# SyncE's program of a graph network's three score passes, written out without its loop

## What is computed

```python
# layer 0: attention logits for 4 heads
a = einsum('ehd,ehd->eh', q[src], k[dst]) / sqrt(32)      # then a softmax over the edges of dst
# layer 1: an edge weight from a small network
h = gelu(concatenate([x[src], x[dst]]) @ mlp_w1 + mlp_b1)
edge_weight = sigmoid(h @ mlp_w2 + mlp_b2)
# layer 3: additive attention for 4 heads
e = leaky_relu(e_l[:, src] + e_r[:, dst], 0.2) + log(clip(w))
# all: out = segment_sum(weight * value[src], dst)
```

## Time and profile before

| what | value |
|---|---|
| median of three runs | 8695.56 us |
| profiled execution, its own time | 8723.79 us |
| its span | 8722.0 us |
| first, second, third score pass | about 121 to 1476, 2175 to 3491 and 6870 to 8201 us of the span |
| busy time: POOL, PE, DVE, ACT | 4695.0 us (54%), 3867.5 (44%), 3291.5 (38%), 2042.4 (23%) |
| granted TensorE clock over the span | 0.641 of full speed |
| DMA queue of SyncE (hardware_dynamic, q1) | 798344 packets, 452.32 MB |
| DMA queue of GpSimd (software_dynamic, q0) | 159744 packets, 356.39 MB |

### The profile page before, as it was taken

The page is one execution under the profiler, slowest core; times in us unless marked ns, Lnnn a source line. Parts: engine busy times, 40 slices in busy tenths (PEclk is TensorE's granted clock), DMA queues, the critical chain, the costliest instruction groups (busy, mean ns, idle before and its releaser), DMA issues. The chain is left out here.

```text
span 8722.0 us, 99954 instructions
## 1 busy us (share of the span) xinstructions
PE 3867.5 (44%) x22250; PEld 3542.3 (41%) x22250; DVE 3291.5 (38%) x8047; ACT 2042.4 (23%) x3881; POOL 4695.0 (54%) x5007
## 2 busy tenths in 40 slices
PE   4333333463666666666433333433333444444356
PEld 2333333352556555565332323422323433433246
DVE  4222223776344444776322222322222311111376
ACT  1000000583333333897000000000000200000067
POOL 2656564350666666232466666466665356665344
PEclk8666666796665666778656556655555655555589
DMA  5555554351444444564111111111111233333244
GB/s 148 162 161 166 161 158 134 96 154 34 125 123 125 123 126 123 173 196 137 44 45 45 45 45 41 48 44 45 46 44 39 58 83 84 88 85 83 61 125 140
DMA packets 973113, 863.79 MB, mean 99 GB/s; under 512 B 350004, under 2 KB 837256, under 8 KB 972808
## 3 DMA queue, kind: packets, MB, share of 16 engines
q1 hardware_dynamic: 798344, 452.32, 18.8%
q0 software_dynamic: 159744, 356.39, 15.8%
q10 hardware_dynamic: 14976, 54.53, 1.9%
HBM read 669.20 MB, written 193.56 MB: 99 GB/s over the span
## 5 line engine op out<-in xcount | busy, mean ns | idle before, releaser
L774 POOL DMA_INDIRECT sum_rows<-tab_row,sum_idx x1664 | 1578.7, 949 | 631.6 <-issue 551.2
L393 PE MATMUL l_pK<-l_winr,l_hotT 128*128 128x128 f32 (+2 forms) x4992 | 1040.4, 374 | 1774.0 <-ACT l_hotT L435 863.0
L393 PEld LDWEIGHTS l_pK<-l_winr,l_hotT 128*128 128x128 f32 x4992 | 993.2, 304 | 1856.8 <-issue 1412.4
L911 DVE TENSOR_TENSOR acc<-acc,sum_pA 128x128 f32 x4160 | 991.4, 289 | 1949.6 <-DMA att<-in_L_gnn_a_r 894.5
L808 PE MATMUL sum_pA<-sum_hot,sum_rows 128*128 128x128 f32 x3328 | 773.9, 426 | 1678.9 <-DMA sum_rows<-tab_row,sum_idx 1639.9
L808 PEld LDWEIGHTS sum_pA<-sum_hot,sum_rows 128*128 128x128 f32 x3328 | 720.7, 329 | 1732.2 <-issue 874.1
L375 POOL DMA_INDIRECT l_rows<-tab_ax,l_idx x832 | 811.2, 975 | 316.5 <-issue 266.5
L375 POOL DMA_INDIRECT l_rows<-tab_qv,l_idx x832 | 791.5, 951 | 316.4 <-issue 259.6
L375 POOL DMA_INDIRECT l_rows<-tab_wh,l_idx x832 | 789.5, 949 | 316.3 <-issue 278.1
L808 PE MATMUL sum_pA<-sum_hot,sum_wrow 128*128 128x128 f32 x4992 | 723.9, 305 | 358.3 <-DVE sum_hot L261 238.4
L808 PEld LDWEIGHTS sum_pA<-sum_hot,sum_wrow 128*128 128x128 f32 x4992 | 662.6, 214 | 408.4 <-issue 264.3
(11 more groups left out here) (235 smaller groups left out, 4464.9 us busy)
## 6 DMA issues: line engine op xcount, KB each, us to landing
spill<-l_rows SPq DMA_DIRECT2D x312, 512.0 KB
sum_rows<-spill SPq DMA_DIRECT2D x312, 512.0 KB
l_winr<-tab_k SPq DMA_DIRECT2D x840, 64.0 KB
sum_line<-src_lo ACTq DMA_DIRECT2D x104, 512.0 KB, 4.6
l_winr<-tab_b SPq DMA_DIRECT2D x840, 32.0 KB
sum_rows<-tab_row,sum_idx POOLq DMA_INDIRECT x1664
l_winr<-tab_er SPq DMA_DIRECT2D x840, 2.0 KB
l_rows<-tab_qv,l_idx POOLq DMA_INDIRECT x832
```

The costliest lines, as they stand in the source:

```text
L393: last = nc.tensor.matmul(pK[:, b, u, :], hotT[:, b, u, :], winr[:, b * TB + u, :], start=True, stop=True)
L774: nc.gpsimd.indirect_dma_start(rows[:, u, :], None, tab_row, bass.IndirectOffsetOnAxis(idx[:, u:u + 1], 0)).then_inc(s_rows[b], 16)
L911: nc.vector.tensor_tensor(acc[:, u % 2, bass.ds(at, P)], acc[:, u % 2, bass.ds(at, P)], pA[:, b, u, :], ALU.add).then_inc(s_add, 1)
```

## The change

SyncE's program of the score pass is written out for all 104 batches, in the same order. The window starts are read into registers by another call, which gives them as values at once, so that `snap` is gone. Batch numbers are constants when the program is built; so are the address of the store, the place in `base`, and the numbers that all waits compare with. The other engines' programs, the buffers, the DMAs and the semaphores are as they were.

```diff
-                        regs = [sp.alloc_register(L + f"win{u}") for u in range(TB)]
-
-                        def load_windows(n, b):
-
-                            sp.load(regs, base[0:1, bass.ds(n * TB, TB)])
+                        def load_windows(n):
+
+                            b = n % 2
+                            _, at = nc.values_load_multi_w_load_instructions(
+                                base[0:1, n * TB:(n + 1) * TB], engines=[sp.engine], min_val=0, max_val=N,
+                                skip_runtime_bounds_check_because="base holds nodes")
                             sp.wait_ge(s_dst, n + 1)
                             for u in range(TB):
-                                at = sp.snap(regs[u], min_val=0, max_val=N)
-                                sp.dma_start(winr[:, b * TB + u, :], win[bass.ds(at, P), :]).then_inc(s_win[b], 16)
+                                sp.dma_start(winr[:, b * TB + u, :], win[bass.ds(at[u], P), :]).then_inc(s_win[b], 16)
 
-                        def store_values(n, b, i):
+                        def store_values(n):
 
-                            sp.wait_ge(s_rows[b], i * (16 * TB) + 16 * TB)
-                            sp.dma_start(spill[:, bass.ds(n * TB, TB), :], rows[:, b * TB:(b + 1) * TB, v0:v0 + F]
+                            b = n % 2
+                            sp.wait_ge(s_rows[b], (n // 2 + 1) * (16 * TB))
+                            sp.dma_start(spill[:, n * TB:(n + 1) * TB, :], rows[:, b * TB:(b + 1) * TB, v0:v0 + F]
                                          ).then_inc(s_spill[b], 16)
 
-                        load_windows(0, 0)
-                        with sp.Fori(0, ROUNDS) as i:
-                            for b in range(2):
-
-                                load_windows(i * 2 + b + 1, 1 - b)
-                                store_values(i * 2 + b, b, i)
+                        load_windows(0)
+                        for n in range(BATCHES):
+                            load_windows(n + 1)
+                            store_values(n)
```

## The result

The written-out kernel takes 8627.49 us (median; 8620.75 to 8640.22) against 8696.15 us (8670.41 to 8702.45) for the kernel before on the same chip: ratio 0.9926, 95% interval 0.9905 to 0.9947. Faster, by 0.74% where 1.0% was forecast (8608 us). The two medians lie 68.7 us apart, or 0.79%; the 0.74% of the ratio is 64 us.

The account below looks back on a forecast made before the run. The prediction took POOL's waits for late stores and scores, with SyncE and TensorE's signals slowed by gathers, as the bound. Gains of 28, 0 and 59 us, together 87, gave 8695.56 - 87 = 8608 us; range 8430 to 8730.

Parts of the forecast that it names:

- What bounds the kernel: Score passes: during gathers SyncE's instructions crawl and TensorE's signals come late; POOL's wait before its index copy pays.
- The count: SyncE's score-pass program: 5.5 of 31.7 instructions per batch go, worth 0.25 us unhindered, up to 3.9 us hindered.
- The first pass: First score pass: 29 store-ended POOL waits of 6.07 us shrink to the score's 5.09; 28 us gained.
- a store that is no longer late leaves the wait that the score imposes: POOL's store-ended waits fall to the score-ended length: 28 us in the first pass, 59 in the third.
- The third pass: Third score pass: 27 store-ended POOL waits of 5.62 us shrink to the score's 3.43; 59 us gained.
- the rival of the rhythm: Score passes: POOL waits every second batch, always for the score; +27 us, 8722 us; chance 0.22.
- The second pass: Second score pass: no store-ended wait and SyncE itself rests 191.5 us, so 0 us gained.
- its cover being VectorE's L497: Second score pass: VectorE's line L497 covers SyncE's work, so shortening SyncE gains 0 us.
- The total: All three score passes together: 87 us less, from 8695.56 to 8608 us; chance 0.38.
- SyncE's rate as the pass's rate: First and third pass go by SyncE's instruction count; priced at 209 us gained, 8487 us; chance 0.24.
- Code fetch: SyncE's stream: 8187 different instructions must be fetched, stalls cost 218 us, net +131, 8827 us; chance 0.11.
- No effect: SyncE: address helpers and waits return in another form, count stays near 31.7; 8696 us; chance 0.05.

Follow-up runs that it names:

- six instructions put back: Written-out kernel plus six semaphore writes per batch that nobody waits for, after SyncE's first six window loads; 8759.38 us, ratio 1.0064 to the kernel before.

## Why the prediction was right, and where not

**What bounds the kernel: right.** POOL pays in its waits, SyncE and TensorE's signals set their ends, and both hang on the gathers.

**The count: right, the load's length: missed.** 5.5 instructions per batch went; the static store has no register helper, and `snap` was no instruction of its own (the run with the copies kept). But the prediction kept the register load at its 0.74 us without a reason, and it fell to 0.53, in the second pass from 1.00 to 0.53. By the medians that is an estimated 0.2 us per batch in the first and third pass and 0.47 in the second, beside the 0.25 that it gave the 5.5 instructions unhindered. How the gain divides between the two isn't separated.

**The first pass: right in its sum, by luck in its terms.** Forecast 28 us, measured 27. Forecast were 38 waits of 5.09 us each, 193.4 us; measured were 31 of 199.4/31 = 6.43. The waits became fewer and longer: POOL runs 104/31 = 3.4 batches from one to the next, before it was 104/38 = 2.7; that a wait is longer for it is what I take from this, no run varied it alone. The step that failed is "a store that is no longer late leaves the wait that the score imposes", with that wait taken at its old length. And 10 store-ended waits remain, where I wanted few; the longest is still 9.2 us, where the waits of 8 us were to go.

**The third pass: the term that was too large.** Forecast 59 us, measured 44. Here the mean length was right (156.0/45 = 3.47 us against 3.43; 3.60 for the 35 ended by the score) and the number was not: 45 waits, not 40. That goes some way towards the rival of the rhythm, but the score ends a wait in 35 of 104 batches, not in every second. Its own result, no gain, didn't come.

**The second pass: wrong.** Forecast 0, "its cover being VectorE's L497"; measured 17 us, and the run with its loop kept has 1314 us there, as before. SyncE's rest in this pass was no proof that its length was hidden. POOL's waits there fell by 18 us, and this is the pass whose register load got shorter by the most. With the six instructions put back, and the load short, this pass takes 1321 us, so instructions alone can cost time there. That the cover holds for the average batch and not for each is what I take from it; what share of the 17 us the load has, no run tells.

**The total.** 87 us forecast, 88 in the passes of the two profiles: 28 + 59 + 0 against 27 + 44 + 17, so the agreement is luck, one term too large and one left out. Between the runs it is 0.74% or 64 us. The mechanism of the first and third pass stands; against the runs the size was over-read by a third, probably because the terms came from one execution that was 28 us over its median.

**SyncE's rate as the pass's rate (0.24): no.** With 5 instructions per batch for 26.2 the kernel gained another 1.0%, not the hundreds of us that this would give. It comes near to true only with the gathers away: with plain DMAs the looped kernel's SyncE has hardly a wait in the second pass,

```profile
SPq L349 <- DMA l_rows<-tab_ax: 7.1, 14, 0.9
SPq L343 <- PE l_pK L391: 3.6, 2, 3.2
```

and that is the pass in which writing out still gains (29 us, or 0.28 us per batch). POOL's wait for the store in this pass falls by as much, from 141.5 to 112.5 us. That 0.28 lies near the prediction's 0.25 for unhindered instructions doesn't confirm that term, since the register load got shorter as well (the rows above) and SyncE's own waits grew from 10.7 to 76.1 us.

**Code fetch (0.11): no cost seen.** The queues that carry instructions, before and then after (packets, MB, share):

```profile
q14 instruction: 30, 0.25, 0.0%
```

```profile
q14 instruction: 92, 0.75, 0.0%
```

62 packets more, 0.50 MB, and no pass became longer. The Trainium skill (Runtime: NRT & Kernel Launch, Instruction fetch mechanics) has the sequencer fetch the next block of 256 instructions or 16 KiB while it runs the current one. By that page, 8187 instructions are an estimated 32 such blocks, or 0.52 MB. The trace agrees in volume, and with a crossing that is mostly hidden, as far as the length of the passes can tell; gaps at even distances in SyncE's stream were not looked for.

**No effect (0.05):** excluded by the counts, and by the interval.

What the prediction did not have at all is that TensorE, too, waited for windows before the change. In the first pass of the kernel before:

```profile
PE l_pK L393 <- DMA l_winr<-tab_k: 96.7, 16, 12.4
```

It fell to 18.4 us, and looks like a gain. The run with the store first, where it is 249.1 us and the pass as long, shows that it was worth little or nothing.

## What to carry to other kernels

When the engine that pays waits for two things, count which of them ends its waits, and price the removal of the later one by the other; but expect the others' waits to change in number and length, as a pass settles into a new rhythm. Where one queue issues both prefetches and a store that frees a buffer, put the store where nothing stands before it that isn't its own condition: here that was worth nothing beside a heavy queue and 0.6% beside a light one, while the same store on ScalarE, behind its waits, cost 1.9 and 1.5%. Before you shorten a queue's program, pad it: six instructions tell in one run whether its length counts. They do not tell how much a shortening brings; here they cost twice what 5.5 fewer brought. And compare the instructions that stay, too: one of them, the register load, became shorter.

## What the runs showed of the hardware

- While gathers by index are in flight, SyncE's DMA and register instructions take up to some 1400 ns; with plain DMAs from POOL the longest MOVE of the first pass took 35, and the longest window load of the third pass 368 (1317 in the first, at 289 GB/s).
- With gathers ScalarE started 13.2 us after TensorE's last matmul in the piece shown, with plain DMAs 0.12 us. ScalarE's waits in the first pass were 945.0 us of "remote" in the kernel before, and with plain DMAs in its looped program have a named releaser every time:

```profile
ACT l_hotT L434 <- remote: 945.0, 61, 26.9
```

```profile
ACT l_hotT L432 <- PE l_pT L383: 649.2, 104, 17.5
```

- A load of one register from SBUF took 273 ns at the median, one of eight 528 in the written-out program, 742 in the looped one:

```profile
L345 SPq TENSOR_LOAD <-base x315: 14/273/613, 118.0 to 7998.4; - x158
```

The Trainium skill (Runtime: NRT & Kernel Launch, Instruction fetch mechanics) gives about 200 ns per register even in bulk, and speaks of loads from HBM. By that, eight would take an estimated 1600 ns. The loads here read SBUF and took 66 ns for each of the eight, so its figure doesn't carry over to them.
- The same load of eight registers depended on the program around it: with the store on SyncE and the loop, 742 ns at the median, and 891 with plain DMAs; with the loop and the store on ScalarE, 523; in the written-out programs, 528 to 530. No run shows why.
